# Ternary weights by rounding in float32, one operation and one transpose a piece, in new orders

## The reference

```
q = LN(x1) @ Wq + bq;  k, v = LN(ctx) @ Wk + bk, LN(ctx) @ Wv + bv
x = x + softmax(q k^T / sqrt(512)) v @ Wo + bo        # x1 = LN(x)

def bitlinear(x, w):                                  # w: out x in
    scale = clip(mean(|w|, axis=1), 1e-5)             # one scale for each row
    tern = clip(round(w / scale), -1, 1)
    return x @ (tern * scale).T

xn = LN(x)
h = bitlinear(xn, w_fc) + gate * (xn @ v.T @ fast_b.T @ u.T)      # 2048 wide
x = x + bitlinear(relu(h) ** 2, w_proj)
```

## Time and profile before

| | before |
|---|---|
| median of 3 runs | 789.34 us (788.86 to 789.37) |
| the profiled execution | 789.24 us, span 787.4 us |
| instructions | 10870 |

### The profile page before, as it was taken

How to read it: one execution, slowest core, us unless ns; L and a number is a source line. 1 busy time by engine, 2 the same in 40 slices (tenths; PEclk the granted TensorE clock), 3 DMA queues, 4 the chain that set the end, 5 groups by cost and what they waited for, 6 DMA issues and landing times.

```text
span 787.4 us, 10870 instructions
## 1 busy us (share of the span) xinstructions
PE 773.5 (98%) x3877; PEld 645.0 (82%) x3877; DVE 563.1 (72%) x1128; ACT 376.2 (48%) x705; POOL 112.4 (14%) x143
## 2 busy tenths in 40 slices
PE   6999999999999999999999999999999999999997
PEld 4668788888888888888888888888888888888886
DVE  5998886778677687758777687768768687467434
ACT  5997455445443544345443545336443545324332
POOL 3242230110302002110302003110302003010001
PEclk9999999999999999999999999999999999999999
DMA  8743052154211531154210631154130730030101
GB/s 311 278 137 124 7 78 63 41 85 64 107 41 27 90 85 54 41 79 69 87 61 14 101 80 61 41 76 72 55 94 4 104 68 27 0 54 1 55 0 54
DMA packets 180554, 56.93 MB, mean 72 GB/s; under 512 B 167666, under 2 KB 168068, under 8 KB 180500
## 3 DMA queue, kind: packets, MB, share of 16 engines
q1 hardware_dynamic: 150368, 51.51, 26.7%
q10 hardware_dynamic: 30132, 4.73, 3.7%
HBM read 27.64 MB, written 8.39 MB: 46 GB/s over the span
## 4 chain that ended last, share of the span: by engine, by line
PE 94%; DVE 2%; DMA 2%; SPq 1%; issue 0%; ACT 0%; DVEq 0%
PE H L1352 30%; PE O L1333 29%; PE G L1217 25%; PE H L1358 4%; DMA Wv_s<-in_L_xattn_Wv_dram 2%; PE H L1201 1%; PE G L1299 1%; PE O L1406 1%; PE H L1217 1%; PE H L1194 1%; PE O L1373 1%; SPq L520 0%; PE G L1243 0%; PE O L1377 0%; DVE x2a L947 0%
## 5 line engine op out<-in xcount | busy, mean ns | idle before, releaser
L1333 PE MATMUL O<-projT,qbuf 128*128 128x512 f32 x992 | 241.8, 390 | 0.0
L1333 PEld LDWEIGHTS O<-projT,qbuf 128*128 128x128 f32 x992 | 184.8, 188 | 37.6
L780 ACT ACTIVATE rbuf<-H,scf 128x512 f32<-128x512 f32 x128 | 87.7, 686 | 112.3 <-PE H L1358 51.8
L788 ACT ACTIVATE qbuf<-rbuf 128x512 fp32r<-128x512 f32 x125 | 78.6, 629 | 125.0 <-PE O L1333 86.8
L1112 DVE TENSOR_TENSOR qbuf<-rbuf,qbuf 128x512 fp32r<-128x512 f32 x125 | 89.4, 715 | 67.6 <-ACT qbuf L788 66.6
L1352 PE MATMUL H<-even_group,fcT 128*128 128x512 f32 x512 | 126.8, 390 | 0.0
L1352 PE MATMUL H<-odd_group,fcT 128*128 128x512 f32 x512 | 126.7, 390 | 0.0
L1108 DVE TENSOR_TENSOR rbuf<-rbuf 128x512 f32<-128x512 f32 x128 | 95.7, 749 | 32.0 <-ACT rbuf L780 31.9
L1352 PEld LDWEIGHTS H<-odd_group,fcT 128*128 128x128 f32 x512 | 95.5, 188 | 19.5
L1352 PEld LDWEIGHTS H<-even_group,fcT 128*128 128x128 f32 x512 | 95.4, 188 | 19.3
L1217 PE MATMUL G<-Wvo,tT 128*128 128x512 f32 x270 | 63.0, 390 | 0.0
(11 more groups left out here) (196 smaller groups left out, 1015.2 us busy)
## 6 DMA issues: line engine op xcount, KB each, us to landing
xb<-in_x_dram SPq DMA_DIRECT2D x8, 1024.0 KB, 5.1
n_blocks<-n_rows SPq DMA_DIRECT2D x112, 64.0 KB, 2.3
ctxb<-in_ctx_dram SPq DMA_DIRECT2D x8, 768.0 KB, 4.5
n_blocks<-ctxb SPq DMA_DIRECT2D x112, 48.0 KB, 2.1
wring<-in_L_ffn_w_fc_dram SPq DMA_DIRECT2D x16, 256.0 KB, 5.8
...
```

The source lines that it names most:

```text
L780: nc.scalar.activation(rbuf[:, j % 2, :], banks[f"H{j % 2}"][:, :], ACT.Relu, scale=scf[:, j:j + 1]).then_inc(relu_made, 1)
L788: nc.scalar.activation(squares(b, j)[:, HI, :], rbuf[:, j % 2, :], ACT.Copy).then_inc(sqhi_made, 1)
L1333: mm = pe.matmul(banks[f"O{t}"][:, :], qbuf[:, j % 2, h, t * P:(t + 1) * P], projT[:, j, :], start=(j == 0 and h == HI), stop=(j == NFF - ...
```

## The change

A ternary piece becomes one VectorE operation: the piece times the inverse scale, plus 1.5 x 2^23, in float32, which rounds to the nearest whole number (`round:j`). The inverse comes from a reciprocal on VectorE for each group of four (`invert:g`), behind a semaphore of its own. TensorE turns the rounded tile with `pe.transpose` and the float32 identity, four transposes a piece for all 32 pieces. ScalarE stores Sign(bank - 1.5 x 2^23), which is -1, 0 or 1, with the constant as a bias read per partition. The half-scale tiles, the bf16 tiles and the bf16 identity go, as does GpSimd's wait for the rounding. VectorE could also take `abs` words (no list has one), and no piece is stored by VectorE, as before.

```diff
-                        plink(nc.gpsimd.tensor_scalar(sc, asum[:, j, :], 1.0 / D, EPS, ALU.mult, ALU.max))
...
-                        nc.gpsimd.tensor_scalar(half[:, j % 2, 0:n], sc, 0.5, None, ALU.mult)
-                        nc.gpsimd.tensor_scalar(nhalf[:, j % 2, 0:n], sc, -0.5, None, ALU.mult
-                                                ).then_inc(scales_made, 1)
...
-                        nc.scalar.activation(piece_place(j), piece_bank(j), ACT.Copy).then_inc(act_stored, 1)
+                        nc.scalar.activation(piece_place(j), piece_bank(j), ACT.Sign, bias=minus_whole[:, 0:1]).then_inc(act_stored, 1)
...
+                    elif kind == "invert":
+                        dve.wait_ge(scales_made, j + 1)
+                        sc = scf[:, 4 * j:4 * j + 4] if j < 4 else spc[:, j - 4:j - 3]
+                        nc.vector.reciprocal(inverse[:, j % 2, 0:4 if j < 4 else 1], sc).then_inc(inverted, 1)
+                    elif kind == "round":
+                        gr, i = j // 4, j % 4
+                        row = slice(i, i + 1) if gr < 4 else slice(0, 1)
+                        dve.wait_ge(inverted, gr + 1)
+                        if j >= 4:
+                            dve.wait_ge(tern_turned, j - 3)
+                        nc.vector.tensor_scalar(rounded[:, j % 4, :], wring[:, gr % 2, i, :], inverse[:, gr % 2, row],
+                                                WHOLE, ALU.mult, ALU.add).then_inc(rounded_made, 1)
...
                         for k in range(4):
                             cols = slice(k * P, (k + 1) * P)
-                            mm = pe.matmul(banks[f"O{j % 4}"][:, cols], above[:, j % 4, cols], identb[:, :],
-                                           start=True, stop=j in JOINED)
-                            if j in JOINED:
-                                continue
-                            mm = pe.matmul(banks[f"O{j % 4}"][:, cols], below[:, j % 4, cols], identb[:, :],
-                                           start=False, stop=True)
+                            mm = pe.transpose(banks[f"O{j % 4}"][:, cols], rounded[:, j % 4, cols], ident[:, :])
```

More of the change, by code:

```diff
@@ L37 @@
 HI, LO = 0, 1
+WHOLE = 1.5 * 2.0 ** 23
 EPS = 1e-5
@@ L142 @@
     "pe": (
[L143 to L145 removed]
+        "down:0 down:1 up:3 up:4 up:5 down:2 up:6 t:0 t:1 t:2 down:3 down:4 s:0 s:1 up:7 s:2 pT:0 down:5 s:3 down:6 "
+        "pT:1 up:8 up:9 w:0 down:7 w:1 w:2 up:10 a:0 a:1 a:2 a:3 down:8 up:11 up:12 down:9 up:13 down:10 up:14 "
+        "down:11 down:12 up:15 down:13 "
     ).split(),
     "act": (
[4 rows of a table removed]
[4 rows of a table added]
     ).split(),
     "dve": (
[4 rows of a table removed]
[4 rows of a table added]
     ).split(),
     "pool": (
[L160 removed]
+        "residual a:0 a:1 xs23+ a:2 a:3 cs23+ "
     ).split(),
@@ L204 @@
     "sp": (
[3 rows of a table removed]
[3 rows of a table added]
     ).split(),
     "pe": (
[6 rows of a table removed]
[6 rows of a table added]
     ).split(),
     "act": (
[8 rows of a table removed]
[9 rows of a table added]
     ).split(),
     "dve": (
[6 rows of a table removed]
[6 rows of a table added]
     ).split(),
     "pool": (
-        "scale:0 tb xs23 scale:1 cs23 scale:2 scale:3 scale:4 scale:5 residual:0 residual:1 scale:6 residual:2 "
-        "residual:3 scale:7 a:0 a:1 B.xs23 a:2 a:3 B.cs23 "
+        "scale:0 tb scale:1 xs23 scale:2 cs23 scale:3 scale:4 residual:0 residual:1 residual:2 scale:5 scale:6 "
+        "residual:3 scale:7 B.xs23 a:0 a:1 a:2 a:3 B.cs23 "
     ).split(),
 }
-DVE_STORES = [int(word[6:]) for word in PROLOGUE["dve"] if word.startswith("store:")]
-JOINED = [int(word[5:]) for word in PROLOGUE["dve"] if word.startswith("tern:")]
 def prologue_steps(engine):
@@ L290, in mk_xattn_ffn @@
         ident = sb("ident", [P, P])
-        identb = sb("identb", [P, P], BF16)
+        minus_whole = sb("minus_whole", [P, 1])
         tbias = sb("tbias", [P, KC])
         scf = sb("scf", [P, NFF])
-        half = sb("half", [P, 2, 4])
-        nhalf = sb("minus_half", [P, 2, 4])
+        inverse = sb("inverse_scales", [P, 2, 4])
         spc = sb("spc", [P, KD])
@@ L369, in mk_xattn_ffn @@
         fbT4 = sb("fbT4", [RK, 4, RK], F32, setup)
-        above = sb("above", [P, 4, D], BF16, setup)
-        below = sb("below", [P, 4, D], BF16, setup)
+        rounded = sb("rounded", [P, 4, D], F32, setup)
         setup.close()
@@ L404, in mk_xattn_ffn @@
         bq_in, bo_in = sem("bq_in"), sem("bo_in")
-        sides_made = sem("sides_made")
+        rounded_made = sem("rounded_made")
         sprow_made = sem("sprow_made")
@@ L500, in piece_stored, with sums_by @@
         def piece_stored(e, j):
-            mine = j in DVE_STORES
-            e.wait_ge(dve_stored if mine else act_stored, sum((i in DVE_STORES) == mine for i in range(j + 1)))
+            e.wait_ge(act_stored, j + 1)
+        def sums_by(engine, pieces):
+            return sum(f"abs:{j}" in PROLOGUE[engine] for j in range(pieces))
         def squares(b, j):
@@ L843, in steps @@
                         act.wait_ge(ring_in[j % 8], 16 * (j // 8 + 1))
-                        if j >= 2:
-                            act.wait_ge(abs_done, j - 1)
-                        nc.scalar.activation(absj[:, j % 2, :], wring[:, j // 4 % 2, j % 4, :], ACT.Abs,
+                        n = sums_by("act", j)
+                        if n >= 2:
+                            act.wait_ge(abs_done, n - 1)
+                        nc.scalar.activation(absj[:, n % 2, :], wring[:, j // 4 % 2, j % 4, :], ACT.Abs,
                                              accum_out=asum[:, j // 4, j % 4:j % 4 + 1]).then_inc(abs_done, 1)
@@ L1116, in steps @@
                         row = slice(i, i + 1) if gr < 4 else slice(0, 1)
-                        w = wring[:, gr % 2, i, :]
-                        dve.wait_ge(scales_made, gr + 1)
+                        dve.wait_ge(inverted, gr + 1)
                         if j >= 4:
                             dve.wait_ge(tern_turned, j - 3)
-                        if kind == "tern":
-                            link(nc.vector.tensor_scalar(below[:, j % 4, :], w, nhalf[:, gr % 2, row], None, ALU.is_lt))
-                            nc.vector.scalar_tensor_tensor(out=above[:, j % 4, :], in0=w, scalar=half[:, gr % 2, row],
-                                                           in1=below[:, j % 4, :], op0=ALU.is_gt, op1=ALU.subtract
-                                                           ).then_inc(sides_made, 1)
-                            continue
@@ L1127, in steps @@
-                        nc.vector.tensor_scalar(above[:, j % 4, :], w, half[:, gr % 2, row], None, ALU.is_gt)
-                        nc.vector.tensor_scalar(below[:, j % 4, :], w, nhalf[:, gr % 2, row], -1.0, ALU.is_lt, ALU.mult
-                                                ).then_inc(sides_made, 1)
-                    elif kind == "store":
-                        dve.wait_ge(tern_turned, j + 1)
-                        nc.vector.tensor_copy(piece_place(j), piece_bank(j)).then_inc(dve_stored, 1)
+                        nc.vector.tensor_scalar(rounded[:, j % 4, :], wring[:, gr % 2, i, :], inverse[:, gr % 2, row],
+                                                WHOLE, ALU.mult, ALU.add).then_inc(rounded_made, 1)
+                    elif kind == "abs":
+                        dve.wait_ge(ring_in[j % 8], 16 * (j // 8 + 1))
+                        nc.vector.tensor_reduce(asum[:, j // 4, j % 4:j % 4 + 1], wring[:, j // 4 % 2, j % 4, :], AX_X,
+                                                ALU.add, apply_absolute_value=True).then_inc(abs_by_dve, 1)
```

37 lines of the change are left out of this document (19 added, 18 removed), and 87 rows, old and new, of tables (BODY_ORDER, FIRST_ORDER, PROLOGUE).

## The result

| | before | after |
|---|---|---|
| median (11 executions each, measured side by side) | 789.45 us (788.86 to 790.65) | 790.98 us (790.38 to 792.44) |
| ratio | | 1.0021 [1.0013, 1.0030] |
| the profiled execution | 789.24 us, span 787.4 | 792.44 us, span 790.5 |

The changed kernel is slower by 1.5 us, 0.2%. That is little, but clear of the noise (the interval leaves out 1), and the other way than the forecast, which was 788.4 us, 0.9 us faster than before; the time lies inside the stated range, 2.6 us above the forecast.

What follows compares the result with a forecast made beforehand. TensorE, 98% busy, was taken as the bound, with gains only before 98 us. +2.0 - 0.4 - 0.2 - 0.3 - 1.5 - 0.6 = -1.0, 0.1 given back: 789.34 - 0.9 = 788.4 us, range 786.6 to 792.2.

Steps and rivals of the forecast that it cites:

- VectorE: Ternary pieces on VectorE: 33 us of work become 32 rounds of 0.54, 17 us; about 15 us less with the reciprocals.
- small holes of 0.1 us ahead of t:0: -0.2: TensorE just ahead of t:0: its small waits go, saving 0.2 us.
- The part from wvT:0 to t:0: TensorE from the start of wvT:0 to that of t:0: predicted 1.6 us longer.
- Turns: TensorE's 32 turns: 23 pieces keep 0.44 us, nine pay 0.22 us more, +2.0 us, all on the path.
- ScalarE: Stores become Sign with a bias: 703 ns, +0.1 us each, 3 us in all, covered by TensorE, so no path time.
- Start: First loads reordered: M:0 near 17.5 us (+0.4), wvT:0 at 23.1 instead of 23.53, so -0.4 us.
- cs01: Rival: VectorE waits at cs01 for ctx, now the last early load; 790.3 us or up to 791; chance 0.07.
- t:0 to a:0: One turn moved ahead of pT:0: s:0 waits 0.2 us, the hole ahead of pT:0 closes; the part predicted at -0.4 us.
- Tail: Last prologue stretch, a:0 to B.L:0: TensorE's waits for nrm shrink from 1.9 us of holes to 0.4, -1.5 us.
- Bodies: 0: New body orders cost nothing, 0 us; the rival put 0.3 us in each of six, 790.2 us, chance 0.03.
- The clock comes late: Rival: transposes ahead of M:0 do not raise TensorE's clock, its rise comes near 23 us; +3.5, 791.9 us; chance 0.24.

Runs made afterwards that it cites:

- Run 9: Changed kernel with only VectorE's list altered, five rounds moved away from GpSimd's wide operations: 789.60 us, ratio 1.0006 to the kernel before.
- run 4: Changed kernel rounding into bf16 by adding 1.5 x 2^7, each piece turned by four plain bf16 products: 791.09 us, ratio 1.0022 to the kernel before.
- run 5: Orders of the kernel before, with bf16 rounding and plain bf16 products for turns: 788.33 us, ratio 0.9984 to the kernel before.
- run 6: Orders of the kernel before, bf16 rounding, plain bf16 products for turns, ten abs on VectorE: 787.20 us, ratio 0.9974 to the kernel before.
- run 7: Orders of the kernel before, with the change's float32 turns and ten abs moved to VectorE: 789.29 us, ratio 1.0000 to the kernel before.
- Run 1: The change's new operations in the orders of the kernel before: 789.46 us, ratio 1.0001 to the kernel before.
- run 14: Run 9's kernel with the body orders (BODY_ORDER, FIRST_ORDER) of the kernel before: 789.16 us, ratio 0.9999 to the kernel before.
- run 2: Changed kernel with the body orders (BODY_ORDER, FIRST_ORDER) of the kernel before: 791.09 us, ratio 1.0022 to the kernel before.
- run 11: Changed kernel with plain float32 products in place of the transposes of turn:18 and turn:19: 791.18 us, ratio 1.0027 to the kernel before.
- run 10: Changed kernel with the old order of first loads and of first words on TensorE, ScalarE and VectorE: 792.17 us, ratio 1.0037 to the kernel before.
- run 8: Changed kernel with TensorE's scale row moved from ahead of x:2 back behind x:3: 791.31 us, ratio 1.0031 to the kernel before.
- run 13: Changed kernel with rounds 2, 3 and 17 to 19 written as scalar_tensor_tensor instead of tensor_scalar: 792.51 us, ratio 1.0034 to the kernel before.
- run 12: Run 6's kernel with ctx loaded behind Wv, cs01 next to cs23, body 0's normalizing earlier on ScalarE: 786.59 us, ratio 0.9966 to the kernel before.

## Why the prediction was wrong

The failed step is in "VectorE": "32 x 0.54 = 17 us", one price for a round wherever it stands. I took durations from the old trace, in which the half-piece operations happened not to stand beside GpSimd's wide work, and asked of the new order only what it delays in a queue, not what GpSimd runs at the same time. The 32 rounds kept VectorE busy for 19.0 us, 6.8 of them in the five held ones. The consequence is the term "small holes of 0.1 us ahead of t:0: -0.2": there the path got a hole of 0.8 us idle. The part from wvT:0 to t:0 came out +2.4 against my +1.6; with the five rounds moved it is +1.5. Run 9 takes back 1.4 of the 1.5 us between the medians (1.2 us by the two ratios). Its trace puts 0.9 of that on the hole of t:0; 0.3 lies ahead of wvT:0 and goes with an earlier first load of Wq (wqT:0 at 6.38 us against 6.78), which differs from run to run, and what remains, 0.2, may be the clock, which no run separates.

The Trainium skill, "SBUF — State Buffer", Who interferes with whom, says that VectorE and GpSimd arbitrate for one pair of ports as an exclusive lock held for the whole instruction; its practical consequences name tensor_scalar in a two-port mode and operations with two SBUF inputs as those that take part, and leave out other operations with one SBUF input. This case agrees: 1.12 to 1.53 us instead of 0.48 for a round, 1.13 instead of 0.55 for two SBUF inputs, and no longer than without that work for WkT<-H and for the statistics of x, which have one SBUF input each; which mode a round ran in no run shows. It was the page to weigh in the prediction, and I weighed another.

The held rounds are not the whole miss. Against the column of the forecast, run 9, which has none, is still 1.4 us worse: the tail (0.7), the part from t:0 to a:0 (0.6) and the bodies (0.5) each gave less than their terms; the start gave 0.2 more.

By the steps:
- *Turns.* Right: 0.44 us for four transposes, +1.76 us ahead of t:0 (the +1.5 of run 9 with its -0.2 of small holes).
- *ScalarE.* The store is 710 ns (forecast 703), one table load, no time on the path. Right, but I called the engine "covered" where it is level with TensorE: runs 4 to 7 show that it is the second bound of that stage, and that 7 us taken from TensorE buy 1.1 and 6.3 taken from ScalarE nothing.
- *Start.* Right within 0.15 us: M:0 at 17.56 (17.5), wvT:0 at 23.23 (23.1). The two slow rounds there cost little: from wqT:0 to M:0 it is 10.78 us with them and 10.89 in run 9 without.
- *cs01.* As forecast, no cost.
- *t:0 to a:0.* I had -0.4 and run 9 has +0.2. The hole ahead of pT:0 closed, but s:0 waits 0.5 us where I said 0.2, and turns 23 to 25 add 0.5 us of waits that I had not looked for.
- *Tail.* I had -1.5 and -0.4 for the moved turn, the trace has -1.2 in all. The waits for nrm shrank to 0.34 us idle, but with nothing between x:3 and B.L:0 TensorE now waits 0.78 us for ScalarE's evacuation of x:3. Run 1, in the old order, has the same end: VectorE's chain for the four nX sets it.
- *Bodies: 0.* Wrong by 0.5 us (run 14). This was a rival of mine at 0.3 us each and 3 in 100; it came at 0.09 each.
- *The clock comes late*, at 24 in 100. It did not in the profile of the changed kernel: four transposes took 0.85 us from 12.96 to 13.81 and eight took 0.94 us from 15.27 to 16.21, so the higher level (2.4 GHz) came between, ahead of M:0. But in two of the nine profiles with the new start, those of runs 2 and 4, it did: eight transposes at 15.5 us take 1.94 us, and wvT:0 is about 1.5 us later than in the changed kernel (24.70 and 24.68 against 23.23), where I had put 3.5. None of the seven profiles with the old start shows it. The mean granted clock of an execution does not tell (it is 1.000 in run 2's profile), so how much of the median it makes is open.

The Trainium skill, "TensorE: Matmul & The Clock Gate", Part 4: PE-mode transpose, holds that the full clock does not engage for transposes. The traces do not agree: in run 11 the higher level comes ahead of the first plain product, with transposes alone before it. In the profile of the changed kernel it comes some 2 us after the last plain product, bq:0, gave way at 12.96 us. And in run 4, where turn:0 is a plain product, the rise is late all the same. So transposes alone do not account for the late rise; its cause is open.

What the rival had in it and I did not price: the clock can also fall for a moment behind a wait. In the profile of the changed kernel it is at 1.2 GHz from 56.3 to 59.7 us, right behind the hole of t:0, which costs 1.6 us; likewise in runs 4 and 10. Two of eleven executions of the changed kernel have a mean granted clock of 0.998 or less, so its median holds little of this. The cause is not settled. Runs 2, 8 and 13 have the same hole of 0.80 us and no fall, and runs 5, 6 and 12, in the old orders, wait 0.64 to 0.90 us there with none. Run 4 has the fall most often with plain products for turns, so the transposes of the turns are not needed for it.

So the sum of the loss against before: the held rounds 0.9 us by the trace and up to 1.4 by the medians, the bodies 0.4 to 0.5, the rest of the change near nothing. Run 14, with neither, is 789.16 us, and run 1, without the new orders, 789.46: no change.
